# Quantised attention in a transformer forward pass: products signalled by halves, the ones rows made by the rounding's bias, values rounded between the two passes, the projection's bias added on GpSimd

## The chip, the cores and the metric

One core of a Trainium2 chip runs the whole forward pass in one launch. The metric is the device time of the launch in microseconds (us). TensorE is written PE, VectorE DVE, ScalarE ACT, GpSimd POOL, SyncE SP.

## What is computed

The stream `h` has 8 batches of 512 rows with 192 features. Six stages follow one another; the change is in the fourth, an attention whose operands are rounded to 8 bits with one scale per tensor. Cut to what matters:

```python
def fake_quant(x):
    scale = maximum(max(abs(x)) / 127, 1e-8)
    return clip(round(x / scale), -128, 127) * scale

qkv = fake_quant(x) @ fake_quant(w_qkv) + b_qkv        # x: layer norm of h; 12 heads of 16
attn = fake_quant(q) @ fake_quant(k).T * 16 ** -0.5    # per batch and head
attn = fake_quant(softmax(attn))
out = attn @ fake_quant(v)
h = h + fake_quant(out) @ fake_quant(w_proj) + b_proj
```

Each scale is the maximum over a whole tensor, so no rounding can begin before the last batch of what it rounds is known. The scale of the softmax needs the largest probability of all rows, which is why the scores are made twice.

## The kernel before

`quantised_attention` (L1318 to L1927) is written in seven blocks. Inside a block each engine runs its own program in its written order, and semaphores alone tie the engines; between two blocks all five meet at a barrier. A `Signal` is a semaphore with so many increments per batch and some credit given at the start. Queries and keys lie turned (features on partitions): `QF`, `KF` hold for each batch three groups of 512 columns, four heads to a group, each head on 16 of 32 partitions; `QI`, `KI`, `VI` are the rounded values in bf16, in the same memory. `magic` (12582912.0) is the constant whose addition rounds a float32 to an integer.

- **Preparation (L1354 to L1409).** Weights are loaded and rounded, rows are normalised, maxima taken.
- **Products (L1417 to L1551).** Per batch ACT scales x with `magic` as its bias (L1425), DVE subtracts `magic` (`round_x`, L1466), PE turns it (`turn`, L1520), ACT copies it (L1431). PE then makes six products of queries and keys, two matmuls each (L1537, twelve matmuls, six PSUM banks), signals once for all of them, and makes the values in two halves in one further bank (L1527), with `turn(b + 1)` between them. ACT stores three query products, then three key products, with bias (`store`, L1438). DVE stores the two halves of the values (L1474) and takes the maxima of queries, values and keys (L1479, L1482, L1485). The next batch's products wait for both stores.
- **Rounding (L1560 to L1602).** Per batch ACT scales queries, keys and values in turn into two buffers `TM` (L1569), DVE subtracts `magic` (L1582 for queries and keys, L1587 and L1588 for values). POOL clears two buffers of 12 KB per partition beside it (L1593). Behind the last of it SP copies rows of ones into `KI` on partitions 16 to 18 of each group of 32 (L1601, four DMAs of 72 KB): there the second pass multiplies them by a shift that is carried as three bf16 parts in `QI`.
- **First pass (L1616 to L1682).** SP spreads the queries of a batch over a zeroed buffer, four DMAs (L1629), PE makes the scores (L1646), DVE takes row maxima (L1656), POOL turns them into biases (L1666), ACT takes exponentials with row sums `RS` (L1680).
- **Shift (L1701 to L1756).** DVE reduces the row sums, POOL takes the maximum over partitions (L1725), DVE and ACT (logarithm, L1730) make the shift, PE turns it, DVE and ACT copy it to `BT`, and SP writes it into `QI` with twelve DMAs of 24 KB (L1756), behind the spreads of the first two batches (L1697, L1699).
- **Second pass (L1767 to L1856).** 192 units, each two matmuls for scores (L1790), one exponential (L1830), one rounding to bf16 on DVE (L1852) and two matmuls with the values (L1808). ACT may be two exponentials ahead of DVE.
- **Projection (L1863 to L1927).** POOL takes the maximum of the outputs over partitions (L1867). Per batch ACT scales (L1912), DVE rounds (L1883), PE projects (L1925), DVE adds the product to `h` (L1889), adds the bias (L1892) and takes the row statistics for the next stage (L1895, four instructions).

Of the kernel before, what the change touches and what calls it, by code (L numbers as in the profile page):

```python
# [9 lines left out]
BF16 = mybir.dt.bfloat16  # L10
# [7 lines left out]
P = 128  # L18
# [1299 lines left out]
def quantised_attention(nc, m, io):  # L1318
# [17 lines left out]
    magic, AM = m.small(P, [1]), m.small(P, [B, 3])  # L1336
# [10 lines left out]
        "rows_normed"))  # L1347

# [5 lines left out]
    with nc.Block(no_gpsimd_drain=True) as block:  # L1354
        @block.sync
        def _(sp):
# [57 lines left out]
        S1("q_k_products"), S1("q_k_stored", 2), S1("v_products", 2, 3), S1("v_stored", 2)  # L1414
    s_lk, s_mx, s_mr = sem("qa_qkv_chain"), sem("qa_qkv_maxima"), sem("qa_qkv_maxima_of_all")
    batch_of = lambda ap, b: ap[:, bass.ds(b, 1)]
    with nc.Block(no_gpsimd_drain=True) as block:  # L1417
        @block.scalar
        def _(act):
# [14 lines left out]
            def store(b, k):  # L1434
                qk.wait(act, b, 1)
# [73 lines left out]
        def _(pe):  # L1509
# [22 lines left out]
            def batch(b, j, ahead):  # L1532
                xc.wait(pe, b, 1)
                ev.wait(pe, b, 0)
                for s in range(2 * NG):
                    for c in range(NC):
                        ins = pe.matmul(ps[:, 1 + s, :],  # L1537
                                        WQ[:, c, HG * s:HG * s + HG, :].rearrange("p h d -> p (h d)"),
                                        XQT[j][:, c, :], start=(c == 0), stop=(c == NC - 1))
# [14 lines left out]
    tq, rq = Signal(nc, "qa_scaled", 3, 1), Signal(nc, "qa_rounded", 3, 2)  # L1554
    s_on, s_one, s_qz = sem("qa_ones_set"), sem("qa_ones_rows"), sem("qa_spread_zeroed")
    g3 = Cut(m.arena, after, END)
    QM = [Cut(m.arena, X_AT + 12288 * j, C_AT)(P, [NH, S], BF16) for j in range(2)]
    ones = g3(P, [NG * S], BF16)
    TM = [TMP, Cut(m.arena, g3.at, END)(P, [NG * S])]
    with nc.Block(no_gpsimd_drain=True) as block:  # L1560
        @block.scalar
        def _(act):
            tq.start(act)
            with act.Fori(0, B // 2) as i:
                for j, (k, (src, n)) in [(j, kk) for j in range(2) for kk in enumerate(
                        ((QF, NG * S), (KF, NG * S), (VF, T * D)))]:
                    b = 2 * i + j
                    rq.wait(act, b, k - 1)
                    act.activation(TM[(j + k) % 2][:, 0:n], src[:, bass.ds(b, 1), :, :].rearrange(  # L1569
                        "p o x y -> p (o x y)"), ACT.Identity, bias=magic, scale=inv2[:, k:k + 1]  # L1570
                        ).then_inc(tq.sem, 1)

        @block.vector
        def _(v):
            rq.start(v)
            v.memset(ones, 1.0).then_inc(s_on, 1)
            with v.Fori(0, B // 2) as i:
                for j in range(2):
                    b = 2 * i + j
                    for k, dst in enumerate((QI, KI)):  # L1580
                        tq.wait(v, b, k + 1)
                        v.tensor_scalar(dst[:, bass.ds(b, 1), :, :].rearrange("p o g s -> p (o g s)"),  # L1582
                                        TM[(j + k) % 2], MAGIC, None, ALU.subtract).then_inc(rq.sem, 1)
                    tq.wait(v, b, 3)
                    VIb = VI[:, bass.ds(b, 1), :, :, :].rearrange("p o t h d -> p (o t h) d")
                    rounded = TM[j][:, 0:T * D].rearrange("p (h d) -> p h d", d=HD)
                    v.tensor_scalar(VIb[:, :, HD:2 * HD], rounded, 0.0, None, ALU.mult)  # L1587
                    v.tensor_scalar(VIb[:, :, 0:HD], rounded, MAGIC, None, ALU.subtract).then_inc(rq.sem, 1)  # L1588
# [5 lines left out]

        @block.sync
        def _(sp):
            sp.wait_ge(s_on, 1)
            rq.wait(sp, B - 1, 3)
            for j in range(HG):
                rows = slice(32 * j + HD, 32 * j + HD + 3)  # L1600
                sp.dma_start(KI[rows].rearrange("p b g s -> p b (g s)"),  # L1601
                             ones[0:3, None, :].to_broadcast([3, B, NG * S])).then_inc(s_one, 16)  # L1602
# [6 lines left out]
    mark = g3.at  # L1609
    nb = [g3(P, [2]) for _ in range(4)]  # L1610
# [5 lines left out]
    with nc.Block(no_gpsimd_drain=True) as block:  # L1616
# [18 lines left out]
        def _(pe):  # L1635
            sp1.start(pe)
            pe.wait_ge(s_one, 16 * HG)
# [13 lines left out]
        def _(v):  # L1651
            with v.Fori(0, B) as b:
                for n in range(N1):
# [3 lines left out]
                                    ALU.max).then_inc(s_lk, 1)  # L1657

        @block.gpsimd
        def _(pool):  # L1660
            nbs.start(pool)
            for b in range(B):
                for n in range(N1):
# [3 lines left out]
                                       ALU.mult, ALU.mult).then_inc(nbs.sem, 1)  # L1667

# [21 lines left out]
    s_a, s_b, s_c, s_ln, s_bp, s_bt, s_bc, s_q = (sem(f"qa_shift_{n}") for n in (  # L1690
        "chain", "max", "max_of_all", "log", "parts", "turned", "copied", "rows"))
# [8 lines left out]

    with nc.Block(no_gpsimd_drain=True) as block:  # L1701
        @block.vector
        def _(v):
            l = Link(v, s_a)
            l(v.tensor_reduce(pmax, RS, AX.XYZ, ALU.min))
            v.reciprocal(pmax, pmax).then_inc(s_b, 1)
# [6 lines left out]
            for k in range(3):  # L1713
                l(v.tensor_copy(BP[:, :, :, k], W_))
                if k < 2:
# [4 lines left out]
                          ps[0:3 * NH, 0:2, :].bitcast(BF16)).then_inc(s_bc, 1)  # L1720

        @block.gpsimd
        def _(pool):
            pool.wait_ge(s_b, 1)
# [1166 lines left out]
```

## Time and profile before

| | us |
|---|---|
| median of 3 runs (lowest, highest) | 2577.85 (2576.46, 2578.14) |
| the profiled execution's own time | 2583.43 |
| its span, first to last instruction | 2581.4 |
| products, 869.7 to 961 | 91.3 |
| rounding and the wait for the first pass, 961 to 1016 | 55 |
| first pass, 1016 to 1276 | 260 |
| shift, 1276 to 1305 | 29 |
| second pass, 1305 to 1529 | 224 |
| projection, 1529 to 1568 | 39 |

Over the whole span PE is busy 75%, DVE 58%, ACT 41%, POOL 16%. Those shares average over six stages with different limits, so each stretch has to be read by itself. In a timeline a row is: start, time until the last instruction of the row has ended, engine, line, operation, output and input, count, and in brackets the idle time before it and what ended it. "x12" are instructions that follow each other; since an engine overlaps neighbours, starts are a better measure than lengths. POOLq and SPq are what those engines issue. `MODIFY_POOL_CONFIG` is an instruction with which the built program switches POOL between two sets of functions, one for the usual operations and one for the maximum over partitions.

### The profile page before, as it was taken

Reading aid. Unit: us, or ns where it says so; the run is one execution under the profiler, and the core shown is the slowest. Engines: PE = TensorE matmul, PEld = TensorE weight load, DVE = VectorE, ACT = ScalarE, POOL = GpSimd, SP = SyncE. Lnnn points to the kernel's source line nnn. Section 1 sums busy time; section 2 is a strip of 40 time slices with the busy share of each in tenths; the row PEclk is TensorE's granted clock in tenths of the full one; section 3 lists DMA queues with packets and bytes.
Section 4 is the critical chain, followed back from the end, with each engine's and each line's share of the span. In section 5 each row is a group of like instructions: output and inputs, shape, how many; then the busy total and the mean of one; then the engine's idle time right before and its main releaser. Section 6 shows DMA issues by size and latency. Waiting matters only on the chain. (4 is left out here: it accounts for less than half of the span.)

```text
span 2581.4 us, 31194 instructions
## 1 busy us (share of the span) xinstructions
PE 1948.3 (75%) x9560; PEld 1011.4 (39%) x9560; DVE 1506.0 (58%) x2508; ACT 1060.0 (41%) x1847; POOL 405.8 (16%) x592
## 2 busy tenths in 40 slices
PE   5687888868876351777568865788899994899994
PEld 4555645444334120000111123333123332788883
DVE  6376378843003665999757774788968886111113
ACT  2001122222111356999878863222167762222221
POOL 5000000000111000111100002522103335122221
PEclk9899989966886565555589986777589997899997
DMA  3011100051992003433000102977767742566664
GB/s 79 18 31 38 46 23 16 11 222 58 392 411 108 12 0 96 145 118 118 25 18 25 36 0 53 126 110 104 94 79 92 97 61 71 176 204 203 204 204 182
DMA packets 147741, 265.16 MB, mean 103 GB/s; under 512 B 28618, under 2 KB 115883, under 8 KB 142636
## 3 DMA queue, kind: packets, MB, share of 16 engines
q1 hardware_dynamic: 135996, 242.54, 36.3%
q0 software_dynamic: 10480, 18.04, 2.1%
q10 hardware_dynamic: 1152, 3.15, 0.3%
q8 instruction: 62, 1.02, 0.2%
q14 instruction: 51, 0.42, 0.1%
HBM read 221.85 MB, written 57.71 MB: 108 GB/s over the span
## 5 line engine op out<-in xcount | busy, mean ns | idle before, releaser
L1646 PE MATMUL ps<-arena 128*128 x384 | 195.8, 615 | 122.1 <-DMA arena<-arena 62.2
L1680 ACT ACTIVATE ps<-ps,arena 128x512 f32<-128x512 f32 x384 | 257.0, 1456 | 7.7 <-POOL arena L1666 7.7
L2091 DVE TENSOR_REDUCE arena<-ps 128x1024 f32 x192 | 227.7, 1222 | 50.4 <-PE ps L2241 44.4
L1656 DVE TENSOR_REDUCE arena<-ps 128x1024 f32 x192 | 234.7, 1226 | 38.1 <-PE ps L1646 22.1
L1680 ACT ACTIVATION_READ_ACCUMULATOR ps<-ps,arena 128x1 f32 x384 | 239.8, 1002 | 0.0
L2443 ACT ACTIVATE arena<-ps 128x1024 f32<-128x1024 f32 x192 | 185.2, 1022 | 95.7 <-PE ps L2325 94.6
L1830 ACT ACTIVATE arena<-ps 128x1024 f32<-128x1024 f32 x192 | 187.5, 1024 | 33.6 <-DVE arena L1852 29.4
L2773 DVE TENSOR_TENSOR arena<-ps,arena 128x384 f32<-128x384 f32 x39 | 21.8, 558 | 286.8 <-PE ps L2729 286.8
L2241 PE MATMUL ps<-arena 96*128 96x512 bf16 x384 | 159.6, 509 | 37.7 <-DVE arena L2091 25.6
L2753 ACT ACTIVATE arena<-ps,arena 128x256 f32<-128x256 f32 x234 | 89.7, 482 | 235.7 <-PE ps L2718 235.7
L528 PE MATMUL ps<-arena 96*128 96x456 f32 (+1 forms) x512 | 177.2, 500 | 9.6 <-DMA arena<-arena 6.1
L1852 DVE TENSOR_SCALAR arena<-arena 128x1024 bf16<-128x1024 f32 x192 | 130.9, 692 | 68.3 <-ACT arena L1830 67.3
L2729 PE MATMUL ps<-arena 128*128 128x192 f32 x936 | 162.5, 330 | 0.7 <-DVE arena L2773 0.7
L2729 PEld LDWEIGHTS ps<-arena 128*128 128x128 f32 x936 | 151.0, 190 | 13.6 <-issue 13.6
L1646 PEld LDWEIGHTS ps<-arena 128*128 128x128 bf16 x384 | 25.6, 110 | 291.6 <-ACT ps L1680 197.8
L1790 PE MATMUL ps<-arena 128*128 (+1 forms) x384 | 119.7, 395 | 15.2 <-DMA arena<-arena 14.8
L528 PEld LDWEIGHTS ps<-arena 96*128 96x128 f32 x512 | 100.8, 205 | 77.4 <-issue 59.2
L2688 POOL DMA_INDIRECT routed_out<-arena x78 | 74.7, 958 | 283.7 <-DVE arena L2773 271.0
L2714 PE MATMUL ps<-arena 128*128 128x256 f32 x468 | 110.0, 386 | 0.9 <-DVE arena L2767 0.9
L1201 DVE COPY arena<-ps 128x768 f32<-128x768 f32 x16 | 15.3, 958 | 158.0 <-PE ps L1243 158.0
L1808 PE MATMUL ps<-arena 128*32 128x512 bf16 x384 | 76.8, 396 | 40.5 <-DVE arena L1852 33.2
L2391 PE MATMUL ps<-arena 128*32 128x512 f32 x768 | 104.7, 618 | 2.7 <-DVE arena L2468 1.8
(379 smaller groups left out, 3301.4 us busy)
## 6 DMA issues: line engine op xcount, KB each, us to landing
arena<-in_sm_w_dram SPq DMA_DIRECT2D x128, 576.0 KB
arena<-in_re_w_dram SPq DMA_DIRECT2D x39, 1252.0 KB, 5.9
arena<-ra_parts SPq DMA_DIRECT2D x192, 192.0 KB, 9.8
routed_in<-routed_in SPq DMA_DIRECT2D x8, 3332.0 KB, 14.3
ra_parts<-arena SPq DMA_DIRECT2D x48, 192.0 KB, 2.5
arena<-routed_in SPq DMA_DIRECT2D x39, 196.0 KB, 5.3
arena<-la_xt SPq DMA_DIRECT2D x16, 384.0 KB, 3.4
arena<-arena SPq DMA_DIRECT2D x64, 96.0 KB, 2.2
```

The source lines that it names most:

```text
L528: ins = pe.matmul(ps[:, 2 * (t % 2) + bank, to:to + w], XTs[j][:, c, t * P:(t + 1) * P], Wx[:, kind, c, at:at + w], start=(c == 0), stop=( ...
L1646: ins = pe.matmul(ps[:, 2 * (n % 4) + t % 2, :], QM[j][:, h, t * P:(t + 1) * P], KI[:, b, h // HG, :], start=True, stop=True)
L1656: v.tensor_reduce(MXq[:, b, 2 * u:2 * u + 2, at_head(h)], ps[:, 2 * (n % 4):2 * (n % 4) + 2, :], AX.X, ALU.max).then_inc(s_lk, 1)
L1680: ins = act.activation(bank, bank, ACT.Exp, bias=nb[n % 4][:, t % 2:t % 2 + 1], scale=c_reg, accum_out=RS[:, b, t, at_head(h):at_head(h) + 1])
L1790: ins = pe.matmul(ps[:, 2 * (n % 3) + q, :], QM[j][:, h, c * P:(c + 1) * P], QI[:, bass.ds(b, 1), g, :].rearrange("p o s -> p (o s)"), sta ...
L1830: act.activation(PF[n % 2], ps[:, 2 * (n % 3):2 * (n % 3) + 2, :].rearrange("p a s -> p (a s)"), ACT.Exp, scale=c_reg).then_inc(pe_.sem, 1)
L1852: v.tensor_scalar(PB[n % 2], PF[n % 2], MAGIC, MAGIC, ALU.add, ALU.subtract).then_inc(rd.sem, 1)
L2091: v.tensor_reduce(MX[:, bass.ds(b, 1), 2 * (n % 2):2 * (n % 2) + 2, n // 2].rearrange("p o t -> p (o t)"), ps[:, 2 * (n % 2):2 * (n % 2) + ...
L2241: ins = pe.matmul(ps[:, t, :], ST_[j][0][0:KR, h, t * P:(t + 1) * P], ST_[j][1][0:KR, h, :], start=True, stop=True)
L2443: act.activation(PF[e // 2 % 2][:, 2 * (e % 2):2 * (e % 2) + 2, :], ps[:, 2 * (e % 3):2 * (e % 3) + 2, :], ACT.Exp, scale=HD ** -0.5).then ...
L2714: pe.matmul(unit(k), wr[:, k * P:(k + 1) * P], XT[j][:, 0, :], start=True, stop=False)
L2729: ins = pe.matmul(ps[:, 7, h * D:(h + 1) * D], HT[j][:, k, h * P:(h + 1) * P], wr[:, at:at + D], start=(k == 0), stop=(k == KH - 1))
```

## The change

1. The products of queries and of keys are signalled separately (`qk` has two increments per batch). ACT stores the queries after six matmuls, PE's key half waits only for the keys' store of the batch before, and `turn(b + 1)` stands between the two halves.
2. The ones rows are no longer copied by DMA. A second constant, `magic_k`, is `magic` on every partition and `magic` + 1 on partitions 16 to 18 of each group; keys are scaled with it as their bias. Preparation gains two memsets and four DMAs of 12 bytes.
3. In the rounding block batches go in pairs; DVE scales the second batch's keys itself into a third buffer. Only the values of batches 0 and 1 are rounded there. The other six are rounded in the shift block, behind the copies to `BT`.
4. The reduction of `RS` and POOL's maximum over partitions move to the end of the first pass's block. Six of the twelve DMAs with the shift are issued by POOL.
5. The bias of the projection is added to `h` by POOL during the second pass, in a loop of eight, and L1892 goes.

```diff
@@ preparation
             for j in range(HG):
+                one_rows = slice(32 * j + HD, 32 * j + HD + 3)
+                sp.dma_start(magic_k[one_rows], above[0:3]).then_inc(s_one, 16)
...
+            pool.memset(magic_k, MAGIC)
+            pool.memset(above, MAGIC + 1.0)
@@ products: ACT, PE
-                qk.wait(act, b, 1)
+                qk.wait(act, b, k + 1)
...
-                ev.wait(pe, b, 0)
-                for s in range(2 * NG):
...
-                ins.then_inc(qk.sem, 1)
+                for k in range(2):
+                    ev.wait(pe, b, k - 1)
+                    for s in range(NG * k, NG * k + NG):
...
+                    ins.then_inc(qk.sem, 1)
+                    if ahead and k == 0:
+                        turn(b + 1)
                 values(b, j, 0)
-                if ahead:
-                    turn(b + 1)
                 values(b, j, 1)
@@ rounding: ACT
+                for n, (j, src, bias, k) in enumerate(((0, QF, magic, 0), (0, KF, magic_k, 1), (1, QF, magic, 0))):
+                    if n == 0:
+                        rq.wait(act, i, 0)
+                    elif n == 2:
+                        rq.wait(act, i, 1)
+                    act.activation(TM[n % 2], scaled(src, 2 * i + j), ACT.Identity, bias=bias,
+                                   scale=inv2[:, k:k + 1]).then_inc(tq.sem, 1)
+            rq.wait(act, B // 2, 0)
+            for b in range(2):
+                act.activation(TM[b][:, 0:T * D], VF[:, b, :, :].rearrange("p t d -> p (t d)"), ACT.Identity, bias=magic,
+                               scale=inv2[:, 2:3]).then_inc(s_vt, 1)
@@ rounding: DVE
+                rq.wait(v, i, 0)
+                v.tensor_scalar(TM[2], scaled(KF, 2 * i + 1), inv2[:, 1:2], magic_k, ALU.mult, ALU.add).then_inc(s_kt, 1)
+                for n, (j, dst, k) in enumerate(((0, QI, 0), (0, KI, 1), (1, QI, 0), (1, KI, 1))):
...
+                    v.tensor_scalar(scaled(dst, 2 * i + j), TM[n % 2 if n < 3 else 2], MAGIC, None, ALU.subtract
+                                    ).then_inc(rq.sem, 1)
@@ rounding: SP (the block goes)
-                sp.dma_start(KI[rows].rearrange("p b g s -> p b (g s)"),
-                             ones[0:3, None, :].to_broadcast([3, B, NG * S])).then_inc(s_one, 16)
@@ end of the first pass's block: DVE, POOL
+            ex.wait(v, B - 1, N1)
+            l = Link(v, s_a)
+            l(v.tensor_reduce(pmax, RS, AX.XYZ, ALU.min))
+            v.reciprocal(pmax, pmax).then_inc(s_b, 1)
...
+            pool.wait_ge(s_b, 1)
+            pool.partition_all_reduce(pmax, pmax, P, RED.max).then_inc(s_c, 1)
@@ shift: DVE, ACT behind their copies; POOL; SP
+            for b in range(2, B):
+                v.wait_ge(s_vt, b + 1)
+                round_v(v, b, TV[:, b, :].rearrange("p (h d) -> p h d", d=HD))
...
+                act.activation(TV[:, b, :], VF[:, b, :, :].rearrange("p t d -> p (t d)"), ACT.Identity, bias=magic,
+                               scale=inv2[:, 2:3]).then_inc(s_vt, 1)
...
+            pool.wait_ge(s_bc, 2)
+            shift_rows(pool, (2, 3), s_q2)
...
+            shift_rows(sp, (0, 1), s_q)
@@ second pass: POOL; PE
+            with pool.Fori(0, B) as b:
+                Hb = m.H[:, bass.ds(b, 1), :, :].rearrange("p o t d -> p (o t) d")
+                pool.tensor_tensor(Hb, Hb, bp[:, None, :].to_broadcast([P, T, D]), ALU.add)
...
+            pe.wait_ge(s_q, 16 * NG * 2)
+            pe.wait_ge(s_q2, 16 * NG * 2)
@@ projection: DVE
-                v.tensor_tensor(Hb, Hb, bp[:, None, :].to_broadcast([P, T, D]), ALU.add).then_inc(s_e, 1)
-                v.wait_ge(s_e, 3 + b + 1)
```

`round_v` is the pair of L1587 and L1588; `shift_rows` issues the DMAs of L1756 for the groups it is given.

**The order on PE, loop of the products.** The rows before are one batch (L1537 products, L1527 values, L1520 turn):

```order
L1537 MATMUL ps<-arena 128x512 x12
L1527 MATMUL ps<-arena 128x192 x4
L141 REGISTER_ALU
L1520 MATMUL ps<-arena 96x128 x8
L141 REGISTER_ALU
L1527 MATMUL ps<-arena 128x192 x4
```

The same batch now (L1544 products, L1526 turn, L1533 values):

```order
L1544 MATMUL ps<-arena 128x512 x6
L141 REGISTER_ALU
L1526 MATMUL ps<-arena 96x128 x8
L141 REGISTER_ALU
L1544 MATMUL ps<-arena 128x512 x6
L1533 MATMUL ps<-arena 128x192 x4
L141 REGISTER_ALU
L1533 MATMUL ps<-arena 128x192 x4
```

The turn of the next batch has moved from between the halves of the values to ahead of the key half of the products.

**The order on POOL, first pass to projection.** Before (an "ISA" without operands ahead of an operation is a `MODIFY_POOL_CONFIG`; one with operands is the maximum over partitions; a branch leads into or out of a block):

```order
L1666 ISA
L1666 TENSOR_SCALAR arena<-arena 128x2 x192
L1616 UNCONDITIONAL_BRANCH
L1722 UNCONDITIONAL_BRANCH
L1725 ISA
L1725 ISA arena<-arena 128x1
L1701 UNCONDITIONAL_BRANCH
L1864 UNCONDITIONAL_BRANCH
L1867 ISA arena<-arena 128x1
```

And now (L1682 biases, L1685 first maximum, L1723 DMAs of the shift, L1802 the loop's head and end, its own "ISA" being register work, L1804 bias of the projection, L1899 second maximum):

```order
L1682 ISA
L1682 TENSOR_SCALAR arena<-arena 128x2 x192
L1685 ISA
L1685 ISA arena<-arena 128x1
L1629 UNCONDITIONAL_BRANCH
L1747 UNCONDITIONAL_BRANCH
L1723 DMA arena<-arena 3x8x512 x6
L1725 UNCONDITIONAL_BRANCH
L1800 UNCONDITIONAL_BRANCH
L1802 UNCONDITIONAL_BRANCH
L1802 ISA
```

```order
L1804 ISA
L1804 TENSOR_TENSOR arena<-arena 128x768
L1802 REGISTER_ALU
L1802 COMPARE_AND_BRANCH
L1792 UNCONDITIONAL_BRANCH
L1896 UNCONDITIONAL_BRANCH
L1899 ISA
L1899 ISA arena<-arena 128x1
```

The first maximum has moved ahead of a block's end. The bias brings two configurations with it: one ahead of the addition, inside the loop, and one ahead of the second maximum, behind the projection block's entry, where none stood.

## Rows read from the trace of the kernel before

**Rows 1.** Busy time by stretch: length, then each engine, granted clock:
```profile
869.70:961.00 91.30, 55.32 (x224) 25.58 (x224) 49.29 (x55) 47.67 (x64) 0.37 (x1) 0.65 0.00 0
1305.00:1529.00 224.00, 181.14 (x768) 40.96 (x768) 162.09 (x240) 187.55 (x192) 0.00 (x0) 0.97 0.07 21
```

**Rows 2.** Timeline, products: start us, busy us, engine, line, idle before:
```profile
871.35 1.09 PE L1520 MATMUL ps<-arena 128*96 128x128 bf16 x8 [34.79 <-DVE arena L1466]
...
894.65 5.30 PE L1537 MATMUL ps<-arena 96*128 96x512 bf16 x12 [3.23 <-ACT arena L1438]
...
899.75 0.85 PE L1527 MATMUL ps<-arena 96*128 96x192 bf16 x4
...
900.10 2.12 ACT L1438 ACTIVATE arena<-ps,arena 128x512 f32 x3 [4.58 <-PE ps L1537]
...
900.76 0.62 DVE L1474 SCALAR_TENSOR_TENSOR arena<-ps,arena 128x384 f32 x1 [3.76 <-PE ps L1527]
...
902.09 0.62 DVE L1474 SCALAR_TENSOR_TENSOR arena<-ps,arena 128x384 f32 x1 [0.71 <-PE ps L1527]
...
902.62 1.74 DVE L1479 TENSOR_REDUCE arena<-arena  x1
...
905.17 5.30 PE L1537 MATMUL ps<-arena 96*128 96x512 bf16 x12 [3.23 <-ACT arena L1438]
...
906.96 0.55 DVE L1466 TENSOR_SCALAR arena<-arena 128x768 bf16<-128x768 f32 x1
```

**Rows 3.** Timeline of the rounding behind the products:
```profile
961.14 6.06 POOL L1593 MEMSET arena<- 128x3072 f32 x2 [1.73 <-POOLq L1417]
...
964.87 3.15 DVE L1582 TENSOR_SCALAR arena<-arena 128x1536 f32 x1 [0.26 <-ACT arena L1569]
...
968.16 4.14 ACT L1569 ACTIVATE arena<-arena 128x1536 f32 x3 [2.38 <-DVE arena L1582]
...
969.99 0.96 DVE L1582 TENSOR_SCALAR arena<-arena 128x1536 f32 x1 [1.04 <-ACT arena L1569]
...
972.63 4.14 ACT L1569 ACTIVATE arena<-arena 128x1536 f32 x3 [0.33 <-DVE arena L1582]
```

**Rows 4.** Timeline between rounding and first pass, SP and PE:
```profile
1000.37 7.55 SPq L1601 DMA_DIRECT2D arena<-arena  x4
1009.42 4.78 SPq L1629 DMA_DIRECT2D arena<-arena  x4
...
1016.01 3.59 PE L1646 MATMUL ps<-arena 128*128 x8 [62.19 <-DMA arena<-arena]
```

**Rows 5.** The line of the all-reduce between the passes, its instructions:
```profile
L1725 POOLq MODIFY_POOL_CONFIG  x2: 11/11/11, 1276.6 to 1276.6; - x2
```

**Rows 6.** Timeline between the passes:
```profile
1282.32 0.38 POOL L1725 PARTITION_ALL_REDUCE arena<-arena  x1 [8.86 <-issue]
...
1292.33 9.74 SPq L1756 DMA_DIRECT2D arena<-arena  x12
1303.54 1.28 ACT L1830 ACT_TABLE_LOAD   x1 [11.24 <-DVEq L137]
...
1306.22 2.96 ACT L1830 ACTIVATE arena<-ps 128x1024 f32<-128x1024 f32 x3 [1.40 <-PE ps L1790]
```

**Rows 7.** One VectorE line, 1597 to 1603 us, ns min/median/max:
```profile
L2082 DVE TENSOR_SCALAR arena<-arena x4: 368/1040/2175, 1597.8 to 1601.8; 128x192 f32 x4
```

**Rows 8.** GpSimd: an addition of 128x768 elements (ns min/median/max):
```profile
L2595 POOL TENSOR_TENSOR arena<-arena x8: 1819/1828/1832, 1941.4 to 2174.1; 128x768 f32<-128x768 f32 x8
```

**Rows 9.** Costliest groups, second pass: busy us, mean ns, idle before:
```profile
L1852 DVE TENSOR_SCALAR arena<-arena 128x1024 bf16<-128x1024 f32 x192 | 130.9, 692 | 68.3 <-ACT arena L1830 67.3
```

**Rows 10.** Timeline of the projection:
```profile
1529.79 0.35 POOL L1867 PARTITION_ALL_REDUCE arena<-arena  x1 [247.09 <-DVE arena L1875]
...
1541.67 0.96 DVE L1892 TENSOR_TENSOR arena<-arena 128x768 f32 x1
1542.79 1.14 DVE L1895 BATCH_NORM_STATS2 arena<-arena  x4 [0.16 <-DVE arena L1892]
```

More of the change, by code:

```diff
@@ L1335, in quantised_attention @@
     WPf, BQ, bv = TMP[:, 0:NG * D].rearrange("p (g d) -> p g d", g=NG), g2(P, [2 * NG]), g2(P, [D])
-    magic, AM = m.small(P, [1]), m.small(P, [B, 3])
+    magic, magic_k, AM = m.small(P, [1]), m.small(P, [1]), m.small(P, [B, 3])
+    above = m.small(HD, [1])
     sc = m.sc
@@ L1347, in quantised_attention @@
         "rows_normed"))
+    s_one = sem("qa_ones_rows")
     def quant_scale(link, v, am, scl, inv):
@@ L1533, in batch @@
                 xc.wait(pe, b, 1)
-                ev.wait(pe, b, 0)
-                for s in range(2 * NG):
[L1536 to L1539, printed above, removed]
-                ins.then_inc(qk.sem, 1)
+                for k in range(2):
+                    ev.wait(pe, b, k - 1)
+                    for s in range(NG * k, NG * k + NG):
+                        for c in range(NC):
+                            ins = pe.matmul(ps[:, 1 + s, :],
+                                            WQ[:, c, HG * s:HG * s + HG, :].rearrange("p h d -> p (h d)"),
+                                            XQT[j][:, c, :], start=(c == 0), stop=(c == NC - 1))
+                    ins.then_inc(qk.sem, 1)
+                    if ahead and k == 0:
+                        turn(b + 1)
                 values(b, j, 0)
-                if ahead:
-                    turn(b + 1)
                 values(b, j, 1)
@@ L1562, in _ @@
         def _(act):
-            tq.start(act)
+            act.wait_ge(s_one, 16 * HG)
             with act.Fori(0, B // 2) as i:
[L1565 to L1571, printed above, removed]
+                for n, (j, src, bias, k) in enumerate(((0, QF, magic, 0), (0, KF, magic_k, 1), (1, QF, magic, 0))):
[9 more added lines that the diff above has]
+                               scale=inv2[:, 2:3]).then_inc(s_vt, 1)
         @block.vector
@@ L1575, in _ @@
             rq.start(v)
-            v.memset(ones, 1.0).then_inc(s_on, 1)
+            v.wait_ge(s_one, 16 * HG)
             with v.Fori(0, B // 2) as i:
[L1578 to L1588, printed above, removed]
+                rq.wait(v, i, 0)
+                v.tensor_scalar(TM[2], scaled(KF, 2 * i + 1), inv2[:, 1:2], magic_k, ALU.mult, ALU.add).then_inc(s_kt, 1)
+                for n, (j, dst, k) in enumerate(((0, QI, 0), (0, KI, 1), (1, QI, 0), (1, KI, 1))):
+                    if n < 3:
+                        tq.wait(v, i, n + 1)
+                    else:
+                        v.wait_ge(s_kt, i + 1)
+                    v.tensor_scalar(scaled(dst, 2 * i + j), TM[n % 2 if n < 3 else 2], MAGIC, None, ALU.subtract
+                                    ).then_inc(rq.sem, 1)
+            for b in range(2):
+                v.wait_ge(s_vt, b + 1)
+                round_v(v, b, TM[b][:, 0:T * D].rearrange("p (h d) -> p h d", d=HD))
         @block.gpsimd
@@ L1609, in quantised_attention @@
     mark = g3.at
+    s_a, s_b, s_c, s_ln, s_bp, s_bt, s_bc, s_q = (sem(f"qa_shift_{n}") for n in (
+        "chain", "max", "max_of_all", "log", "parts", "turned", "copied", "rows"))
     nb = [g3(P, [2]) for _ in range(4)]
@@ L1689, in quantised_attention @@
     rows = lambda a: a.rearrange("p b t h -> p (b t) h")
-    s_a, s_b, s_c, s_ln, s_bp, s_bt, s_bc, s_q = (sem(f"qa_shift_{n}") for n in (
-        "chain", "max", "max_of_all", "log", "parts", "turned", "copied", "rows"))
+    s_q2 = nc.alloc_semaphore("qa_shift_rows_pool")
+    TV = QF.rearrange("p b g s -> p b (g s)")[:, :, 0:T * D]
     km = [sem(f"qa_k_spread{j}") for j in range(2)]
@@ L1699, in spread, with shift_rows @@
         sp.dma_start(VS[j], VI[:, b, :, :, :]).then_inc(km[j], 16)
+    def shift_rows(eng, groups, done):
+        for q in groups:
+            for g in range(NG):
+                row, at = 32 * q + HD, 3 * (q * NG + g)
+                eng.dma_start(QI[row:row + 3, :, g, :], BT[at:at + 3, :, :]).then_inc(done, 16)
     with nc.Block(no_gpsimd_drain=True) as block:
@@ L1733, in _ @@
                            ps[0:3 * NH, 2:4, :].bitcast(BF16), ACT.Copy).then_inc(s_bc, 1)
+            for b in range(2, B):
+                act.activation(TV[:, b, :], VF[:, b, :, :].rearrange("p t d -> p (t d)"), ACT.Identity, bias=magic,
+                               scale=inv2[:, 2:3]).then_inc(s_vt, 1)
         @block.tensor
@@ L1752, in _ @@
             sp.wait_ge(s_bc, 2)
-            for q in range(HG):
-                for g in range(NG):
-                    row, at = 32 * q + HD, 3 * (q * NG + g)
-                    sp.dma_start(QI[row:row + 3, :, g, :], BT[at:at + 3, :, :]).then_inc(s_q, 16)
+            shift_rows(sp, (0, 1), s_q)
     g5 = Cut(m.arena, mark, END)
```

32 lines of the change are left out of this document (14 added, 18 removed).

## The prediction

> **What bounds the kernel now.** The chain that ended last covers only the final stage, so I read the stretches of this stage one by one: first the busy times by stretch, then the timeline of each, then groups and single lines for prices.
>
> In the products [rows 1] no engine is busy for more than 61% of 91.3 us, so a loop of waits sets the pace. The timeline [rows 2] shows it: PE's twelve matmuls start at 894.65 and again at 905.17, a period of 10.5 us. ACT sat idle for 4.58 us until they were done, and PE for 3.23 us until ACT had stored. The matmuls run at 5.10 / 12 = 0.425 us each, which for 512 columns is 1.2 GHz; the granted clock of the stretch is 0.65.
>
> In the rounding ACT and DVE take turns over two buffers: a batch costs 972.63 - 968.16 = 4.47 us [rows 3]. Then comes the copy of the ones rows: SP issues from 1000.37, the next block's spreads leave at 1009.42, and the first scores start at 1016.01, on a DMA [rows 4]. The first pass is ACT's and I leave it alone. Between the passes POOL's maximum comes 5.7 us after its configuration, and the second pass begins after twelve DMAs and a table load [rows 5, 6]. The second pass makes 192 units in 224 us, less 1.2 before the first exponential and some 3 after the last: 1.14 each, near ACT's pace, which is busy for 187.55 of them [rows 1]. In the projection DVE runs nearly without a break.
>
> **The change part by part**, in us, minus is faster. Durations are of the profiled execution, whose own time was 2583.43 at a span of 2581.4; the median of the runs shown is 2577.85, 5.6 lower than the former, and I carry differences over to it.
>
> *Preparation: 0.* Four small DMAs put four issues on SP ahead of the later weight loads, 3.2 in all at the 0.8 of SP's other small copies [rows 6]. DVE asks for the weights only behind the rows and maxima of eight batches, which hides that; without this cover it would cost the 3.2. POOL's two memsets lie beside the same work.
>
> *Products: +1.8.* The handover by halves removes PE's wait on ACT. But the turn now stands between the halves and waits for DVE's rounding of x, which follows all of DVE's work on the batch before. That closes a new loop, in starts [rows 2]: rounding to turn 0.6 (0.55 and a semaphore), turn 1.1, six matmuls 2.55, values to DVE's first store 900.76 - 899.75 = 1.0, to its second 1.3, to the first reduction 0.5, three reductions and back to the rounding 906.96 - 902.62 = 4.35 less 0.15 of waiting. Sum 11.3 against 10.5. ACT's 47.67 / 8 = 6 per batch fit in [rows 1]. PE would still be idle for 3 to 4 us in one piece, so I keep its clock. Six batches lose 0.8, and the last wins back some 3: its products are ready while DVE still reduces batch 6, where DVE now waits 3.8 for twelve matmuls. Net +1.8; ends -10 (the clock, below) and +5 (nothing won back).
>
> *Rounding: -4.8.* For a pair of batches ACT has three operations, starts 1.54 apart and each 1.65 long; DVE subtracts 0.18 later [969.99 against 968.16 + 1.65, rows 3], twice in 1.89, and ACT resumes some 0.15 after: 3.08 + 1.65 + 0.18 + 1.89 + 0.15 = 6.9, where two batches took 8.9. The keys that DVE scales itself hide under ACT's first operation, whether they take 0.96 or nearly twice that. The first pair meets POOL's clearing: one subtraction took 3.15 for 0.96, ending after POOL did [rows 3]. DVE has one more operation there now, so I add 3.1. Four pairs 27.7 + 3.1, then the values of two batches, 3.4: 34.2, against 39.0 from 961.3 to 1000.3.
>
> *Ones rows: -9.7.* From DVE's end at 1000.3 to the first scores took 15.7 [rows 4]. Without the copies a block's entry costs at most the 1.5 from SP's last copy to the first spread, I take 1.0; four issues of 0.8 take 3.2; and the scores follow the last issue by 1.8, as now [rows 4]: 6.0. Ends -9 and -11.
>
> *Between the passes: -1.4.* POOL's configuration can follow its last bias, at 1282.32 - 8.86 = 1273.5, so the maximum is ready 5.7 later, at 1279.2 [rows 5, 6]. It is late even so, and the block's end waits for it. The new block starts near 1280.2, and the logarithm needs a table load of 1.28 that was hidden before: 1281.5, against about 1282.9. Ends 0 and -3.
>
> *Shift to second pass: -3.4.* Let R be the end of ACT's copy (1292.3 now). The second pass's first exponential comes at R + 13.9 [rows 6]. SP's six DMAs take 4.9. The values of six batches cost ACT 1.0 each and DVE twice 0.55, the time of the 768 elements of L1466 [rows 2]; they end at R + 7.4, which is what comes last. Add the 1.5 from 1302.07 to the table load at 1303.54, and its 1.28: R + 10.2. For POOL's six DMAs there is no row; the bounds are 0.8 each, as on SP, and all behind DVE's rounding, with first scores near R + 13. I take R + 10.5, nearer to SP's row, and keep 0 and -4.
>
> *Second pass: +10.* This is the largest price. POOL adds the bias eight times, 1.83 each alone [rows 8]. A DVE operation from SBUF to SBUF with a constant did not run beside POOL's work: besides the 3.15 above, one of 0.37 took 2.175 beside two POOL additions [rows 7]. L1852 is of that kind, 0.692 [rows 9]. If the two alternate, a unit takes 1.83 + 0.69 + 0.1 = 2.6 for eight units: 8 x (2.6 - 1.14) = 11.7, less some 1.5 since DVE's work on the outputs can hide. Ends 0 (no conflict) and +14 (POOL's part 2.175). That the eight may be spaced by configurations changes little: each still stops DVE once, for about 1.2.
>
> *Projection: -2.3.* L1892 and its wait leave DVE: from 1541.67 to 1542.79 is 1.12 [rows 10], of which the wait before the statistics keeps 0.12, so 8 x 1.0 = 8.0. ACT's loop, 1.65 + 0.96 + 0.3, stays below what is left. But in the program a configuration now stands inside this block ahead of the second maximum, which before came as soon as DVE's reduction was done [rows 10]. At the one measured price it comes 5.7 later [rows 5, 6]. Ends -8 and -1.
>
> Sum: 1.8 - 4.8 - 9.7 - 1.4 - 3.4 + 10 - 2.3 = -9.8. 2577.85 - 9.8 = 2568.
>
> **A rule against the change.** In the rows POOL's clearing and DVE's subtraction ran one behind the other [rows 3]; a plain copy issued by POOL beside such work is not in them. The Trainium skill, "SBUF — State Buffer", "SBUF: two separate sides", says in its box on the "DVE blocks DMA" trap that POOL cannot write the descriptors of its DMAs while a DVE operation of this kind runs, and that the queues of ACT and SP are free of it. By that rule the term of -3.4 would be near 0.
>
> **The rivals.**
> *A, no conflict in the second pass.* For it: POOL has 224 us for 15 us of work, and DVE is idle for 62 of them [rows 1]. Against: rows 3 and 7. 2568 - 10 = 2558.
> *B, PE's clock stays up in the products.* Turn, key half and values would take 2 less per batch, so six loops give 12: 2556. For it: PE's work is more evenly spread. Against: a gap of over 3 us remains, and behind such a gap the matmuls run at 0.425 now [rows 2].
> *C, POOL's DMAs come late.* The term of -3.4 is gone: 2571.4.
> *D, slower.* If the configuration in the loop costs 5.7 each time, the additions stretch over 8 x 7.6 = 61 us. If each stop of DVE also lets PE's clock fall to 1.2 GHz, a unit needs four matmuls of 0.425, 1.7 instead of 1.14, and the stretch loses 61 x (1 - 1.14 / 1.7) = 20 more: 2588. It comes out slower than before from 10 on, half of the 61 us at the low clock. Against it: the clock is 0.97 in this pass [rows 1], and the rows hold no repeated configuration. The Trainium skill, "GPSIMD Engine Reference", "2.1 Instruction dispatch", puts some 6 us on the first call after a load of functions; the one price here agrees with 5.7, and no row shows the same set loaded again.
>
> **How the numbers follow.** My forecast has a chance of 0.57 and its own range 2561 to 2576. A has 0.16, B 0.08, C 0.14, D 0.05. A measurement of this kernel can tell 0.2%, 5.2 us, from no change. Below 2572.7 lie A, B, most of C (0.09) and 0.85 of my own case (0.48): 0.81. Above 2583 lies D, 0.05. The rest, 0.14, is between. The range reaches from B to the upper end of my own case and C: 2555 to 2577.
>
> **What would show it.** Right: a product period near 11.3 with PE's turn (L1526) waiting for DVE's rounding (L1472); first scores some 6 us after the rounding; the first maximum 5.7 after POOL's last bias; eight roundings L1884 of 2 us or more early in the second pass; the second maximum 6 us after its block's entry; each batch of the projection 1.0 shorter. Wrong: no long L1884 (A), a product period below 10 (B), a second pass that starts on POOL's DMAs (C), a low granted clock in the second pass (D).

## The result and the profile after

| | before | after |
|---|---|---|
| median of 20 runs each, on the same chips (lowest, highest), us | 2577.19 (2569.52, 2583.54) | 2571.57 (2565.29, 2578.68) |
| ratio, 95% interval | | 0.998 (0.9972 to 0.9989) |
| span of the profiled execution, us | 2581.4 | 2569.6 |

The change saves 5.6 us, where 9.8 were forecast. The interval, a gain of 0.11% to 0.28%, does not reach zero, but the gain is as small as the 0.2% that the prediction took as the least that can be told. I cut both profiled executions at instructions that both kernels have: the first row of a stretch in the timeline, or the last of the one before. Stretches in us:

| stretch | before | after | difference | forecast |
|---|---|---|---|---|
| preparation | 29.79 | 29.88 | +0.1 | 0 |
| products, up to the two memsets of the rounding | 91.47 | 93.90 | +2.4 | +1.8 |
| rounding, up to DVE's last one | 39.14 | 34.49 | -4.65 | -4.8 |
| from there to the first scores | 15.73 | 5.64 | -10.1 | -9.7 |
| first scores to the logarithm | 266.91 | 263.65 | -3.3 | -1.4 |
| logarithm to the end of ACT's copy | 9.38 | 9.72 | +0.3 | 0 |
| from there to the first exponential of the second pass | 13.92 | 12.22 | -1.7 | -3.4 |
| second pass | 223.29 | 233.34 | +10.05 | +10 |
| projection, up to the next stage's first DMA | 38.76 | 37.14 | -1.6 | -2.3 |
| the stage | 728.39 | 719.98 | -8.4 | -9.8 |

The stages ahead of it and behind it took 3.4 less in this execution, with the same code; over all kernels of this study the part ahead lies between 834.7 and 842.6. So what the two profiles show of the change is the stage's -8.4; why the medians have 2.8 less is not shown, but single executions of one kernel differ by 13 us. How well a stretch repeats matters for what follows. Preparation, rounding and the stretch from the logarithm to ACT's copy repeat within 0.03 wherever their code is the same. Other stretches do not: the changed products took 91.0, 91.1, 92.8, 93.0 and 93.9 in the five executions that have them unaltered (granted clock 0.63, 0.63, 0.61, 0.61 and 0.59), the first pass up to the logarithm 263.1 to 264.1, and the second pass with POOL's additions 231.8 to 233.3. There is one profile of the kernel before.

**Products.** Timeline of after, 884 to 903 us (start, busy, engine, line, idle before and its releaser; read as [rows 2]):

```profile
884.75 1.09 PE L1526 MATMUL ps<-arena 128*96 128x128 bf16 x8 [4.18 <-DVE arena L1472]
...
895.56 0.55 DVE L1472 TENSOR_SCALAR arena<-arena 128x768 bf16<-128x768 f32 x1
...
896.16 1.09 PE L1526 MATMUL ps<-arena 128*96 128x128 bf16 x8 [2.91 <-DVE arena L1472]
...
897.04 2.77 PE L1544 MATMUL ps<-arena 96*128 96x512 bf16 x6
...
899.61 0.85 PE L1533 MATMUL ps<-arena 96*128 96x192 bf16 x4
...
900.62 0.62 DVE L1480 SCALAR_TENSOR_TENSOR arena<-ps,arena 128x384 f32 x1 [4.51 <-PE ps L1533]
```

The turn waits for DVE's rounding, DVE waits 4.51 for the values: each is idle while the other works. The period is 896.16 - 884.75 = 11.4, forecast 11.3. Between the other turns of the loop it is 10.7 to 11.4, shorter where a part of PE's work ran at the higher clock. Busy times by stretch, products (as [rows 1]):

```profile
869.70:961.00 91.30, 55.43 (x220) 26.27 (x218) 47.83 (x54) 48.22 (x63) 0.37 (x1) 0.59 0.00 0
```

The granted clock is 0.59, no higher than the 0.65 before.

**Rounding and the start of the first pass.** Timeline of after, 961 to 1001 us (as [rows 3, 4]):

```profile
961.26 6.06 POOL L1613 MEMSET arena<- 128x3072 f32 x2 [1.73 <-POOLq L1423]
...
961.74 2.98 DVE L1598 TENSOR_SCALAR arena<-arena 128x1536 f32 x1 [1.03 <-DVEq L137]
964.65 4.35 DVE L1604 TENSOR_SCALAR arena<-arena 128x1536 f32 x2
...
972.10 4.78 ACT L1585 ACTIVATE arena<-arena 128x1536 f32 x3 [2.14 <-DVE arena L1604]
972.14 1.08 DVE L1598 TENSOR_SCALAR arena<-arena 128x1536 f32 x1 [0.20 <-DVE arena L1604]
...
...
979.01 4.78 ACT L1585 ACTIVATE arena<-arena 128x1536 f32 x3 [2.13 <-DVE arena L1604]
...
996.43 3.12 SPq L1642 DMA_DIRECT2D arena<-arena  x4
...
1001.39 3.59 PE L1658 MATMUL ps<-arena 128*128 x8 [47.37 <-DMA arena<-arena]
```

A pair takes 979.01 - 972.10 = 6.91. Two DVE operations are drawn out in the first pair, L1598 to 2.98 for 1.08 and one of L1604 to 3.5 for 0.96, and each ends 0.8 after one of POOL's two clearings does. Before each later pair ACT still waits 2.13 for DVE.

**Between the passes.** Timeline of after, 1262 to 1287 us, and the line of the first maximum (as [rows 5, 6]):

```profile
1262.15 1.28 ACT L1755 ACT_TABLE_LOAD   x1 [1.14 <-PEq L1629]
...
1264.44 0.38 POOL L1685 PARTITION_ALL_REDUCE arena<-arena  x1 [5.96 <-issue]
1264.85 0.15 DVE L1730 TENSOR_SCALAR arena<-arena 128x1 f32<-128x1 f32 x1 [3.06 <-POOL arena L1685]
...
1265.04 0.61 ACT L1755 ACTIVATE arena<-arena 128x384 f32<-128x384 f32 x1 [1.60 <-DVE arena L1730]
...
1272.89 1.87 ACT L1757 ACTIVATE arena<-ps 36x2048 bf16<-36x2048 bf16 x1 [7.23 <-PE ps L1771]
1274.66 5.61 ACT L1760 ACTIVATE arena<-arena 128x768 f32<-128x768 f32 x6
1274.79 4.94 SPq L1723 DMA_DIRECT2D arena<-arena  x6
1275.06 3.58 POOL L1723 DMA_DIRECT2D arena<-arena  x6 [10.24 <-ACT arena L1757]
...
1282.59 1.28 ACT L1862 ACT_TABLE_LOAD   x1 [2.32 <-DVEq L137]
...
1285.91 2.74 PE L1822 MATMUL ps<-arena 128*128 128x512 bf16 x6 [13.06 <-DMA arena<-arena]
...
1286.98 2.96 ACT L1862 ACTIVATE arena<-ps 128x1024 f32<-128x1024 f32 x3 [3.11 <-PE ps L1822]
```

```profile
L1685 POOLq MODIFY_POOL_CONFIG  x2: 11/11/11, 1258.7 to 1258.7; - x2
```

The line of the shift's DMAs, SP's part of it, and who waited for it (us, times):

```profile
L1723 SPq DMA_DIRECT2D arena<-arena x6: 760/761/862, 1274.8 to 1279.0; - x6
...
  PE ps L1822: 13.1, 1
```

The maximum comes 5.7 after its configuration, as forecast. But the next block begins at 1262.15, 2.3 before it: the block's end does not wait for it. Behind the copy (R = 1274.76) the table load is done at R + 9.1, and PE starts at R + 11.15, released by a DMA. It is one of SP's: of POOL's six, asked in the same way, the trace names nobody who waited. SP's last issue begins at 1279.0, so its transfer was there 6.9 later.

**Second pass.** Its costliest group on the page of after (busy us, mean ns, idle before; as [rows 9]), the line of the additions, the timeline, and two rows by stretch:

```profile
L1884 DVE TENSOR_SCALAR arena<-arena 128x1024 bf16<-128x1024 f32 x192 | 142.7, 756 | 55.8 <-ACT arena L1862 54.5 <-PE ps L1840 1.2
```
```profile
L1804 POOLq MODIFY_POOL_CONFIG  x16: 7/8/11, 1282.4 to 1304.7; - x16
L1804 POOL TENSOR_TENSOR arena<-arena x8: 1911/2179/2182, 1289.5 to 1304.8; 128x768 f32 x8
```
```profile
1292.06 1.02 ACT L1862 ACTIVATE arena<-ps 128x1024 f32<-128x1024 f32 x1 [0.54 <-DVE arena L1884]
1294.28 1.02 ACT L1862 ACTIVATE arena<-ps 128x1024 f32<-128x1024 f32 x1 [1.20 <-DVE arena L1884]
1296.49 1.02 ACT L1862 ACTIVATE arena<-ps 128x1024 f32<-128x1024 f32 x1 [1.20 <-DVE arena L1884]
```
```profile
1300.00:1310.00 10.00, 7.44 (x21) 1.17 (x20) 9.85 (x8) 4.93 (x5) 6.82 (x4) 0.50 0.00 0
...
1312.00:1320.00 8.00, 6.51 (x31) 1.49 (x30) 6.36 (x10) 6.93 (x8) 0.00 (x0) 1.00 0.01 2
```

While POOL adds, a unit takes 2.22 instead of 1.14, DVE looks busy for 9.85 of 10 us with its roundings drawn out to 2.3, and PE's granted clock falls from 1.00 (1291 to 1294) to 0.50 (1.2 GHz). The unit from 1292.06 to 1294.28 took 2.22 at the full clock already, so the low clock is not what makes a unit long. The last addition ends at 1304.8 + 2.2 = 1307.0, and from 1312 on the clock is 1.00.

**Projection.** Timeline of after (as [rows 10]):

```profile
1520.32 0.18 DVE L1907 TENSOR_REDUCE arena<-arena 128x1 f32<-128x24 f32 x1 [0.58 <-PEq L1792]
1526.04 0.38 POOL L1899 PARTITION_ALL_REDUCE arena<-arena  x1 [219.10 <-issue]
1526.45 0.15 DVE L1353 TENSOR_SCALAR arena<-arena 128x1 f32<-128x1 f32 x1 [5.96 <-POOL arena L1899]
...
1532.84 1.01 DVE L1921 SCALAR_TENSOR_TENSOR arena<-ps,arena 128x768 f32 x1
...
1535.92 1.01 DVE L1921 SCALAR_TENSOR_TENSOR arena<-ps,arena 128x768 f32 x1
```

POOL's maximum starts 5.72 after DVE's reduction, where it started 0.28 after it before (1529.79 [rows 10] against 1529.51): 5.4 later than it could. A batch takes 3.08 in the rows shown.

### The profile page after: what moved, and what is told of

Its sections match the earlier page's. It is cut to its first block and busy times, and to the rows that moved or that the text cites. A ratio compares the mean times of both kernels' runs of the same rounds, so it can differ in the third digit from the quotient of the medians.

```text
span 2569.6 us, 31209 instructions
## 1 busy us (share of the span) xinstructions
PE 1952.4 (76%) x9560; PEld 1008.4 (39%) x9560; DVE 1513.8 (59%) x2503; ACT 1054.7 (41%) x1843; POOL 427.4 (17%) x608
## 5 line engine op out<-in xcount | busy, mean ns | idle before, releaser
L528 PE MATMUL ps<-arena 96*128 96x456 f32 (+1 forms) x512 | 172.0, 489 | 9.0 <-DMA arena<-arena 5.5
L1884 DVE TENSOR_SCALAR arena<-arena 128x1024 bf16<-128x1024 f32 x192 | 142.7, 756 | 55.8 <-ACT arena L1862 54.5
```

The lines of the kernel that those rows point to most:

```text
L528: ins = pe.matmul(ps[:, 2 * (t % 2) + bank, to:to + w], XTs[j][:, c, t * P:(t + 1) * P], Wx[:, kind, c, at:at + w], start=(c == 0), stop=( ...
L1884: v.tensor_scalar(PB[n % 2], PF[n % 2], MAGIC, MAGIC, ALU.add, ALU.subtract).then_inc(rd.sem, 1)
```

## The experiments

Each starts from the changed kernel. Its stretches are cut at the same instructions; "after" stands for the values of the table above.

**1. The turn back between the halves of the values.** The signals by halves stay.

```diff
                     ins.then_inc(qk.sem, 1)
-                    if ahead and k == 0:
-                        turn(b + 1)
                 values(b, j, 0)
+                if ahead:
+                    turn(b + 1)
                 values(b, j, 1)
```

> Against the changed kernel, the turn of the next batch stands again between the two halves of the values; the signal by halves stays. Theory (a loop through DVE's rounding of x, the turn and the key half sets the period of 11.4 us): the loop is open, PE's own work of some 8.5 us at 1.2 GHz sets the pace, and the products go from 92.2 us to about 72; if PE's clock rises as well, to 62. Rival (the lower granted clock of the stretch, 0.59 against 0.65, or the cost of signalling twice, made it slower): the stretch stays above 88. All else unchanged.

Measured: 2546.04 (2542.38 to 2550.81), ratio to the kernel before 0.9874 (0.9854 to 0.9894). The products take 65.49 instead of 93.90, every other stretch is as in after within 0.9. Busy times by stretch and timeline of this kernel, products:

```profile
872.00:938.00 66.00, 41.05 (x224) 20.48 (x224) 47.93 (x55) 47.70 (x64) 0.37 (x1) 0.84 0.00 0
```
```profile
903.21 0.65 PE L1526 MATMUL ps<-arena 128*96 128x128 bf16 x8 [1.21 <-DVE arena L1472]
...
905.14 1.47 PE L1544 MATMUL ps<-arena 96*128 96x512 bf16 x6 [0.89 <-ACT arena L1437]
909.72 0.65 PE L1526 MATMUL ps<-arena 128*96 128x128 bf16 x8 [0.86 <-DVE arena L1472]
```
```profile
904.40 0.62 DVE L1480 SCALAR_TENSOR_TENSOR arena<-ps,arena 128x384 f32 x1 [0.71 <-PE ps L1533]
```

So the loop is the turn's place: from one turn to the next 6.5 to 7.0 here, 10.7 to 11.4 in after. PE's longest wait inside the loop is 1.22, the granted clock 0.84, and six matmuls take 1.47 instead of 2.77 wherever the clock is up, which is so in most batches and not in all. The products are shorter than opening the loop gives at the low clock (72), and longer than with everything at the high clock (62). In the batch shown DVE is idle for 0.71 of 6.5 us, so it now comes near to setting the pace. Signalling by halves was worth 26 us in the products (91.47 to 65.49, the higher clock included), and the turn's place took 25.5 to 28.4 of them back, by the five executions of the closed loop.

**2. and 3. The bias elsewhere.** Back on DVE in the projection:

```diff
-        @block.gpsimd
-        def _(pool):
-            with pool.Fori(0, B) as b:
...
-                pool.tensor_tensor(Hb, Hb, bp[:, None, :].to_broadcast([P, T, D]), ALU.add)
@@ projection
                 hh.wait(v, b, 1)
+                v.tensor_tensor(Hb, Hb, bp[:, None, :].to_broadcast([P, T, D]), ALU.add).then_inc(s_e, 1)
+                v.wait_ge(s_e, 3 + b + 1)
```

> The projection's bias is added by DVE again, and POOL's loop in the second pass goes; all other parts of the change stay. Theory (POOL's additions and DVE's roundings exclude each other, and the configuration in front of the second maximum is on the path): first exponential to the last reduction of the second pass goes from 233.3 us to 223.3, the projection from 37.1 to 38.8; in sum 8.3 faster. Rival (the second pass is longer because it starts with PE at the low clock, or because of where its DMAs fall): it stays above 230, and the kernel is 2 us slower.

Or on POOL still, but in the block of the products:

```diff
@@ products
         def _(pool):
+            with pool.Fori(0, B) as b:
+                Hb = m.H[:, bass.ds(b, 1), :, :].rearrange("p o t d -> p (o t) d")
+                pool.tensor_tensor(Hb, Hb, bp[:, None, :].to_broadcast([P, T, D]), ALU.add)
             pool.wait_ge(s_mx, 1)
@@ second pass
...
-                pool.tensor_tensor(Hb, Hb, bp[:, None, :].to_broadcast([P, T, D]), ALU.add)
```

> POOL adds the bias during the products, where it is otherwise idle and DVE works mostly on PSUM and in reductions, and not in the second pass. Theory: second pass 223.3 as without POOL; no second configuration behind it, so the projection takes 37.1 - 5.7 = 31.4; in the products one or two roundings of x wait for an addition, 0 to 4 us. In sum 12 to 15.7 faster than the changed kernel. Rival (DVE's reductions and stores are blocked too): products 8 x 1.1 or more longer.

| | after | bias on DVE | on POOL, in the products |
|---|---|---|---|
| ratio to before | 0.998 | 0.9956 (0.9938 to 0.9973) | 0.9928 (0.9902 to 0.9953) |
| median, us (not of the same chips throughout; the ratios compare) | 2571.57 | 2565.80 | 2557.74 |
| products | 93.90 | 92.82 | 91.83 |
| second pass | 233.34 | 224.94 | 224.85 |
| projection | 37.14 | 39.43 | 31.69 |

The additions cost the second pass 8.4, and win 2.3 in the projection: the bias' move is a loss of 6. The rival of the first of the two, a second pass above 230 without them, is out. The projections with and without L1892, neither with a late maximum, differ by 39.43 - 31.69 = 7.7, or 0.97 a batch. Groups of the kernel with the bias on DVE, and the additions' line in the kernel with the bias in the products:

```profile
L1878 DVE TENSOR_SCALAR arena<-arena 128x1024 bf16<-128x1024 f32 x192 | 130.9, 692 | 59.1 <-ACT arena L1856 58.0 <-PE ps L1834 1.1
```
```profile
L1513 POOLq MODIFY_POOL_CONFIG  x16: 1/2/11, 868.4 to 888.7; - x16
L1513 POOL TENSOR_TENSOR arena<-arena x8: 1792/1798/2036, 875.4 to 888.8; 128x768 f32 x8
```

Without them the rounding is back at 692 ns. In the products an addition takes 1.80, 2.18 in the second pass; one DVE rounding of 0.55 takes 1.10 there, and the stretch, 91.83, lies within the 91.0 to 93.9 of the kernels without additions in it.

**4. POOL's maximum called once more behind the additions,** on a value that nobody reads then, so that the change of functions falls into the second pass:

```diff
                 pool.tensor_tensor(Hb, Hb, bp[:, None, :].to_broadcast([P, T, D]), ALU.add)
+            pool.partition_all_reduce(am, am, P, RED.max)
```

> POOL's additions stay in the second pass, and behind them it takes one more maximum over partitions of a scratch value, so that the configuration falls into the second pass and none stands in the projection. Theory: the second maximum is ready as soon as DVE's reduction is, and the projection takes 37.1 - 5.7 = 31.4 us; the second pass stays at 232 to 234. Rival (the first maximum after a long idle time is slow whatever stands ahead of it): the projection stays at 37.

One run: 2559.78. Projection 31.69, 5.45 less; second pass 232.52. Timeline of this kernel, projection:

```profile
1515.81 0.37 POOL L1900 PARTITION_ALL_REDUCE arena<-arena  x1 [206.91 <-DVE arena L1908]
```

The maximum now waits for DVE alone. The +5.7 of the forecast, 5.45 here, is the change of functions.

**5. DVE's rounding of the values behind POOL's DMAs.** This tells whether POOL's DMAs are late because DVE works beside them.

```diff
+            v.wait_ge(s_q2, 16 * NG * 2)
             for b in range(2, B):
```

> A probe, slower on purpose: DVE's rounding of the six values in the shift block waits until POOL's six DMAs have landed. Theory (C of the prediction, DVE's rounding holds up what POOL needs for its DMAs): they land 2 to 3 us after issue instead of 5.0 in the median, and DVE's rounding begins within 6.5 us of the end of ACT's copy. Rival (a DMA issued by POOL is simply slow to start): the landing stays near 5.0 and DVE begins 9 us or more after ACT's copy.

One run: 2577.54. Timeline and DMA line of this kernel (the last row is issue to landing):

```profile
1275.66 3.58 POOL L1723 DMA_DIRECT2D arena<-arena  x6 [10.24 <-ACT arena L1758]
1285.20 0.56 DVE L1572 TENSOR_SCALAR arena<-arena 128x768 bf16<-128x768 f32 x1 [12.20 <-DMA arena<-arena]
```
```profile
L1723 POOL DMA_DIRECT2D arena<-arena x6: 563/566/782, 1275.7 to 1278.7; - x6
...
DMA to landing us min/median/max: 2.4/5.0/6.5
```

With DVE idle POOL issues its six in 3.58 and they land after 5.0 in the middle and 6.5 at most: the same three numbers as in after. The last is there 9.8 after R. So the rival came, and the lateness is not DVE's doing. The rows of after show a sign of the conflict on the other engine only: while POOL issued, five of DVE's roundings took 0.62 to 0.64 instead of 0.55. That the rule of the forecast (the Trainium skill, "SBUF — State Buffer", "SBUF: two separate sides", the box on the "DVE blocks DMA" trap) acts here is not shown by either kernel. In after PE starts at R + 11.15, 1.3 later than DVE does here after its wait for POOL's six. Those 1.3 are SP's: its own six transfers are the last to land, as the line under "Between the passes" shows.

**6. All twelve DMAs on SP.**

```diff
-            pool.wait_ge(s_bc, 2)
-            shift_rows(pool, (2, 3), s_q2)
...
-            shift_rows(sp, (0, 1), s_q)
+            shift_rows(sp, (0, 1, 2, 3), s_q)
```

> All twelve DMAs of the shift are issued by SP again, beside the rounding of the six values by ACT and DVE. Theory (the second pass waits for the last landing, and a DMA of POOL's takes up to 6.5 us to land with or without DVE beside it): SP's last issue begins 9 us after ACT's copy and lands 4 us later, the first exponential comes 14 us after the copy, where the changed kernel has 12.2. Rival (the values' rounding is what the pass waits for): it stays at 12.2 or less.

One run: 2569.91. From R to the first exponential 14.16, where after takes 12.22 and before 13.92. Timeline of this kernel:

```profile
1272.40 9.94 SPq L1723 DMA_DIRECT2D arena<-arena  x12
...
1285.45 0.13 PEld L1816 LDWEIGHTS ps<-arena 128*128 128x128 bf16 x2 [15.25 <-DMA arena<-arena]
```
```profile
L1723 SPq DMA_DIRECT2D arena<-arena x12: 770/770/867, 1272.4 to 1281.6; - x12
```

The split between the queues is the whole gain of the shift, 1.9; that the values are rounded in the same time costs 0.2 at most (14.16 against the 13.92 of before). The last of twelve on SP alone is there 1285.45 - 1281.6 = 3.9 after its issue begins, SP's last of the split 6.9 after: the split ends the issuing 5.0 earlier and the landing only 2. That the transfers of the two queues hold each other up would fit this; no run tests it.

**7. What the experiments point to.** The turn as in 1, the bias as in 3, and in the rounding a credit more, since the next pair's first scaling writes the buffer that the third of the four subtractions has read, and need not wait for the fourth:

```diff
-    tq, rq = Signal(nc, "qa_scaled", 3, 0), Signal(nc, "qa_rounded", 4, 1)
+    tq, rq = Signal(nc, "qa_scaled", 3, 0), Signal(nc, "qa_rounded", 4, 2)
...
                     if n == 0:
-                        rq.wait(act, i, 0)
+                        rq.wait(act, i, -1)
```

> Three edits on the changed kernel: the turn between the halves of the values, POOL's additions during the products, and in the rounding block ACT's first operation of a pair no longer waits for the last subtraction of the pair before (one more credit), which frees 0.93 us of its 2.1 us of idle time per pair. Theory: products 65 to 70 (65.5, and up to three roundings of x behind an addition), rounding 34.5 - 3 x 0.93 = 31.7, second pass 225, projection 31.7; in sum 44 faster than the changed kernel at best and 39 at worst, near 2530. Rival (the savings overlap, or POOL's additions stall the products, now near DVE's pace): products above 75.

Measured: 2529.86 (2518.46 to 2533.01), ratio to the kernel before 0.9802 (0.9783 to 0.9821). Rounding 31.89, products 67.86, second pass 224.41, projection 31.68. The products are 2.4 longer than in experiment 1, where POOL did not add: once the loop is open, the additions may not be free there. With one profile of each, that is not told from what this stretch varies by. Timeline of this kernel, rounding:

```profile
949.70 4.79 ACT L1588 ACTIVATE arena<-arena 128x1536 f32 x3 [1.27 <-DVE arena L1607]
...
955.74 4.79 ACT L1588 ACTIVATE arena<-arena 128x1536 f32 x3 [1.26 <-DVE arena L1607]
```

A pair takes 6.04, 0.87 less than in after. The stage is 51.5 shorter than before the change, the medians of the same chip 47.5.

## Why the prediction was right, and where it was not

The time of 2571.57 lies in the range, 3.6 above the forecast. The likeliest case came: a small gain, eaten in the products and the second pass. Two steps of the working failed, between the passes and in the shift, and it is luck that they cancel.

- **Preparation, 0.** +0.1. Right.
- **Products, +1.8.** +2.4 between the two profiles, but -0.4 to +2.4 over the five executions of the changed products, +0.9 in the mean; the size of so small a term is not shown. The new loop, its members and its period (11.3, measured 10.7 to 11.4) were right, and experiment 1 shows the cause: with the turn back, 25.5 to 28.4 us go. Rival B's premise, a more even PE, did not hold while the loop stood: PE waited up to 4.18, and only a part of the matmuls ran at the higher clock.
- **Rounding, -4.8.** -4.65. A pair at 6.9 and a first pair 3.1 longer were right.
- **Ones rows, -9.7.** -10.1. The four issues took 3.12, at 0.8 each.
- **Between the passes, -1.4.** -3.3. This step failed: "It is late even so, and the block's end waits for it." The next block began without the result. The blocks are opened with `no_gpsimd_drain=True` (L1629), which I had not weighed; that this is why was not tried. ACT loaded its table beside it (1262.15), so the logarithm came 0.2 after the maximum was ready and not 1.0 + 1.28.
- **Shift, -3.4.** -1.7, and the logarithm's stretch +0.3. This step failed too: the values' rounding "is what comes last". It was out of the way, with the table load done at R + 9.1. What came last was the landing of SP's own six DMAs, at R + 11.15, which I had priced by their issues alone (4.9). POOL's six, for which I had taken R + 10.5 and kept a rival, issue faster than SP's (0.56 against 0.76) and were there by R + 9.8. The first exponential came at R + 12.2. Rival C (R + 13.9) is out as a mechanism: the pass did start on DMAs, but not on POOL's, and DVE does not delay those (experiment 5). Why the transfers of the split land so much later after their issue stays open. The two errors, between the passes 1.9 more gain than forecast and here 2.0 less, cancel.
- **Second pass, +10.** +10.05 between the two profiles, but 8.4 and 8.5 between the experiments with and without the additions. The other 1.6 are not theirs: without additions the pass took 224.4 to 224.9 in three kernels and 223.29 in before, and the same code differs by as much from one execution to the next. So the hit of +10 is luck in part. Eight units at 2.22 are 8 x (2.22 - 1.14) = 8.6; I had 2.6, less a 1.5 that I thought DVE could hide. The conflict and its place were right, the unit 0.4 too long, and nothing was hidden. Rival A is out: the roundings took 2.3.
- **Projection, -2.3.** -1.6. Both parts were right in size: taking the addition away was worth 7.7 (forecast 8.0), and the late maximum cost 5.45 (forecast 5.7).
- **Rival D** is out. The loop issues its configuration again for each addition; the first addition comes 7.1 after the first configuration, then they follow each other without a gap. The Trainium skill, "GPSIMD Engine Reference", "2.1 Instruction dispatch", with its some 6 us for the first call after a load, agrees with 5.7 where the set changes; here the same set again cost nothing. D's other half was partly true: the clock did fall to 0.50, but while POOL adds a unit of 2.22 is longer than the 1.7 of four matmuls at that clock, and it was back some 4 us behind the last addition.

The sum of -9.8 against -8.4 in the stage is, beside the two that cancel, mainly the products' 0.6 and the projection's 0.7. The 2.8 by which the medians show less, -5.6, are not explained by any step of the forecast.

## What to carry to other kernels

When one engine's instruction is moved ahead of another, list what it waits for before listing what it frees: the turn moved between the halves made every batch a chain of PE, DVE and PE again, and hid a gain of 26 us behind a loss as large. Work on GpSimd is free only beside VectorE work that it does not stop, so the same eight additions cost 8.4 in one block and nothing that can be told in another, and a change of its functions belongs where nobody waits for it. When transfers are split over two queues, count until they land and not until they are issued. A forecast that comes out right by its sum can hold two wrong terms of opposite sign, so compare it stretch by stretch.

## What the runs showed of the hardware that I had not expected

- A block's end did not wait for POOL's maximum over partitions: the next block ran 2.3 us before the result.
- POOL issued a DMA of 24 KB in 0.56 us against SP's 0.76. Its six landed up to 6.5 us after their issue, with DVE busy or idle, and SP's last beside them after 6.9, where the last of twelve on SP alone took 3.9.
- POOL's addition and DVE's rounding excluded each other, but not to the last tenth. Beside other work they take 1.80 and 0.69, in sum 2.5; a unit of both took 2.22. The Trainium skill, "SBUF — State Buffer", "Who interferes with whom", calls the ports that the two engines share "an exclusive lock". The drawn-out roundings of 2.3 agree; the 2.22 is 0.3 less than the sum. DVE's own roundings of 0.55 begin 0.47 apart where nothing stops them, so a part of each duration overlaps its neighbour's anyway; whether more than such ends ran side by side is not shown.
- The granted clock was 0.84 in the products of experiment 1, where PE's waits inside the loop were at most 1.2 us, against 0.59 in after, where they were 3 to 4: as many matmuls in less time.
